# A ConvLSTM recurrence on one core: one sigmoid per half-step, and input products for row pairs

## The reference

```python
# layer 0: masked convolution, recurrence over the 16 image rows, skip
h = conv(x, w_i2s * mask)            # 1x3 kernel, 96 -> 192 channels, then a channel shuffle
for each image row:
    s = conv1d(_h, w_s2s) + h_row    # 1x3, 48 -> 192
    o, f, i, g = split(sigmoid(s), 4)
    c = f * c + i * g
    _h = o * tanh(c)
x = x + conv(out_h, w_skip * mask) + b_skip
# layer 1: tokens (16 x 256 x 96)
t = t + attention(layernorm(t))      # 6 heads of 16, causal, whole images of 256 tokens
t = t + moe(layernorm(t))            # 4 experts, hidden 384, gelu, the best 2 of 4
```

## Time and profile before

| | |
|---|---|
| median of three runs | 463.71 us |
| the profiled execution | 465.41 us, span 463.4 us |
| mean granted TensorE clock | 0.985 of full |
| PE busy | 436.8 us, 94% |
| PE weight loads | 347.5 us, 75% |
| DVE busy | 270.1 us, 58% |
| ACT busy | 263.8 us, 57% |
| POOL busy | 147.4 us, 32% |

### The profile page before, as it was taken

One profiled execution on the slowest core, in us unless ns is written; L12 is line 12 of the kernel. 1 busy time (PEld: TensorE's weight loads), 2 busy tenths in 40 slices (PEclk: granted clock), 3 DMA queues, 4 the chain that ended last, 5 costly groups with the idle time before them and its releaser, 6 DMA issues.

```text
span 463.4 us, 10793 instructions
## 1 busy us (share of the span) xinstructions
PE 436.8 (94%) x3186; PEld 347.5 (75%) x3186; DVE 270.1 (58%) x954; ACT 263.8 (57%) x740; POOL 147.4 (32%) x311
## 2 busy tenths in 40 slices
PE   6999998878799999999999999999999999999997
PEld 6999996445578777777786787678777876787776
DVE  3888888457417752774377348635852676166324
ACT  2544444246486648555855675576648664865370
POOL 5000000525503621553155315432542362245100
PEclk9999999969999999999999999999999999999899
DMA  8500000210021012101200210021002001200000
GB/s 211 124 0 0 0 0 1 64 39 18 25 47 35 0 40 52 31 0 46 54 20 0 52 50 17 0 59 43 17 7 75 20 0 34 54 16 1 18 2 18
DMA packets 14409, 14.95 MB, mean 32 GB/s; under 512 B 5426, under 2 KB 11316, under 8 KB 14388
## 3 DMA queue, kind: packets, MB, share of 16 engines
q1 hardware_dynamic: 13940, 14.15, 12.0%
q10 hardware_dynamic: 256, 0.39, 0.3%
q0 software_dynamic: 192, 0.15, 0.2%
HBM read 3.86 MB, written 1.57 MB: 12 GB/s over the span
## 4 chain that ended last, share of the span: by engine, by line
PE 75%; DVE 12%; ACT 6%; issue 4%; POOL 1%; DMA 1%; DVEq 1%; ACTq 1%; SPq 0%; POOLq 0%
PE F L1044 19%; PE T L1002 9%; PE A L1023 8%; PE F L1060 4%; PE F L1064 4%; PE S L986 4%; PE F L1061 3%; PE S L988 3%; PE F L1040 3%; PE S L991 2%; DVE c L647 2%; DVE ig L645 2%; ACT tc_sb L483 2%; DVE pt_sb L469 1%; PE M L965 1%
## 5 line engine op out<-in xcount | busy, mean ns | idle before, releaser
L420 POOL TENSOR_SCALAR p_sb<-p_sb,rden 128x128 f32<-128x128 f32 (+1 forms) x192 | 79.8, 430 | 130.8 <-DVE rden L728 128.6
L1044 PE MATMUL F<-w_sb,hid 128*128 128x96 f32 x768 | 102.3, 278 | 0.0
L1044 PEld LDWEIGHTS F<-w_sb,hid 128*128 128x128 f32 x768 | 94.7, 194 | 6.0 <-issue 6.0
L530 ACT ACTIVATE p_sb<-S,nmax 128x128 f32<-128x128 f32 (+1 forms) x192 | 78.9, 425 | 13.9 <-DVE nmax L722 13.8
L722 DVE TENSOR_REDUCE nmax<-S 128x2 f32<-128x512 f32 (+1 forms) x80 | 50.7, 633 | 48.7 <-PE S L991 48.4
L469 ACT COPY pt_sb<-T 128x512 f32<-128x512 f32 (+1 forms) x48 | 26.4, 550 | 68.5 <-PE T L1002 68.5
L576 ACT ACTIVATE hid<-F,b_sb 128x512 f32<-128x512 f32 x72 | 49.3, 686 | 8.1 <-PE F L1064 7.5
L1023 PE MATMUL A<-pt_sb,v_cur 128*32 128x128 f32 x576 | 44.2, 284 | 8.5 <-ACT pt_sb L469 4.5
L1002 PE MATMUL T<-id_sb,p_sb 128*128 128x128 f32 x288 | 49.4, 290 | 1.4 <-POOL p_sb L420 1.4
L1002 PEld LDWEIGHTS T<-id_sb,p_sb 128*128 128x128 f32 x288 | 30.9, 143 | 16.5 <-issue 13.9
L986 PE MATMUL S<-k_bd,q_st 96*128 96x384 f32 (+2 forms) x96 | 39.1, 414 | 3.2 <-DMA k_bd<-k_cur 2.5
(11 more groups left out here) (148 smaller groups left out, 794.3 us busy)
## 6 DMA issues: line engine op xcount, KB each, us to landing
k_bd<-k_cur SPq DMA_DIRECT2D x93, 32.0 KB, 2.0
q_st<-q_cur SPq DMA_DIRECT2D x28, 96.0 KB, 2.2
k_bd<-k_cur SPq DMA_DIRECT2D x93, 16.0 KB, 1.8
t_st<-t_cm SPq DMA_DIRECT2D x7, 192.0 KB, 2.4
out_y<-y_sb SPq DMA_DIRECT2D x7, 192.0 KB, 1.9
x_pad<-in_x SPq DMA_DIRECT2D x2, 612.0 KB, 8.7
w_sb<-in_w SPq DMA_DIRECT2D x1, 576.0 KB
hid<-in_w SPq DMA_DIRECT2D x1, 576.0 KB, 7.0
```

The source lines that it names most:

```text
L420: last = nc.gpsimd.tensor_scalar(p, p, rden[:, u % 3, i:i + 1], 1.0, ALU.mult, ALU.mult)
L530: last = nc.scalar.activation(p_sb[:, u % 3, i * nk:(i + 1) * nk], S[u % 2][:, i * nk:(i + 1) * nk], ACT.Exp, bias=nmax[:, u % 3, i:i + 1] ...
L1044: last = mm(dst[:, e * C:(e + 1) * C], hid[:, c, s * TT:(s + 1) * TT], w2_sb[:, c], start=False, stop=(c == NCH - 1), skip_group_check=True)
```

## The change

- The gate weights are rearranged while they are loaded, so that a PSUM bank holds g and i on partitions 0 to 47 (groups 0 and 1) and f and o on 64 to 111. This takes four DMAs for the input weights and four for the state weights, plus one for the skip weights; five of the nine are issued by ACT.
- ACT makes the gates of a half-step with one Sigmoid over 112 partitions and 256 columns, in place of two Tanh.
- DVE's part of a half-step is ig, fc, the cell and the two copies of h, all tensor_tensor without constants. fc, the cell and its tanh live on partitions 64 to 111.
- The skip is no longer DVE's: ACT copies it out of PSUM with the bias (`take_skip`), then POOL adds x to it (`add_input`).
- A bank now holds two rows of one half (`pair_bank`). The input's share is made for a pair of rows at once: for each of two gate groups and two taps three single-pass matmuls of 256 columns. For this x is split for each pair: ACT makes the high part (`high_inputs`), POOL the low part (`low_inputs`). The first pair is made in fp32 (`first_inputs`). The input weights are split once.

The diff, cut to its core:

```diff
+        def pair_bank(parity, hb):
+            return G[2 * parity + hb][0:GATE_M, :].rearrange("p (c r n) -> p c r n", c=2, r=2)
+        SWAPS = ((0, slice(FEAT, GATE_M), 0), (1, slice(0, 64), 1))
+        CROSS = ((0, slice(0, FEAT), 1, slice(64, GATE_M)), (1, slice(64, GATE_M), 0, slice(0, FEAT)))
 # sync
-            sp.dma_start(win_sb[:], w_input).then_inc(w_input_in, 16)
+            for blk, cols, blk_from in SWAPS:
+                sp.dma_start(win_sb[:, blk::2, cols], w_input[:, blk_from::2, cols]).then_inc(w_input_in, 16)
...
 # gpsimd
+            def low_inputs(p, parity):
+                pool.wait_ge(x_hi_done, p)
+                nc.gpsimd.tensor_tensor(x_lo[:, parity], pair_rows(p), as_f32(x_hi[:, parity]), ALU.subtract
+                                        ).then_inc(x_lo_done, 1)
+            low_inputs(1, 1)
...
+            def add_input(m, hb, row):
+                pool.wait_ge(skip_taken, m + 1)
+                dst = skip_out(row, hb)
+                nc.gpsimd.tensor_tensor(dst, dst, x_row(row)[:, hb * HALF:(hb + 1) * HALF, 1:], ALU.add
+                                        ).then_inc(t_half, 1)
+            def add_pair(p, parity, first=False, more=True):
+                if not first:
+                    for hb in range(2):
+                        add_input(4 * p - 2 + hb, hb, 2 * p - 1)
+                if more:
+                    low_inputs(p + 2, parity)
+                for hb in range(2):
+                    add_input(4 * p + hb, hb, 2 * p)
 # scalar
+            for blk, cols, blk_from, cols_from in CROSS:
+                act.dma_start(win_sb[:, blk::2, cols], w_input[:, blk_from::2, cols_from]).then_inc(w_input_in, 16)
...
-                nc.scalar.activation(t_fg[:, hb], v[64:64 + FEAT], ACT.Tanh, scale=0.5).then_inc(gates_tanh, 1)
-                nc.scalar.activation(t_ig[:, hb], v[0:FEAT], ACT.Tanh, scale=0.5).then_inc(gates_tanh, 1)
+                nc.scalar.activation(gate[:, hb], src, ACT.Sigmoid).then_inc(gates_done, 1)
...
+            def take_skip(m, hb, row):
+                act.wait_ge(skip_ready, m + 1)
+                nc.scalar.activation(skip_out(row, hb), K[hb][0:C, 0:HC].rearrange("p (b w) -> p b w", w=W), ACT.Identity,
+                                     bias=bsk_sb[:, 0:1]).then_inc(skip_taken, 1)
+            def pair(p, parity, first=False, more=True):
+                for r in range(2):
+                    for hb in range(2):
+                        m = 4 * p + 2 * r + hb
+                        cell_gates(m, hb, pair_bank(parity, hb)[:, :, r])
+                        if not (first and r == 0):
+                            take_skip(m - 2, hb, 2 * p + r - 1)
+                        if more and r == 0 and hb == 0:
+                            high_inputs(p + 2, parity)
+                        cell_out(m, hb)
...
+            act.wait_ge(x_in[2], 16)
+            pair(0, 0, first=True)
 # vector
+            def new_cell(m, hb):
+                dve.wait_ge(gates_done, m + 1)
+                V.tensor_tensor(ig[UP, hb], gate[LOW, hb, 0], gate[LOW, hb, 1], ALU.mult).then_inc(cell_dve, 1)
+                V.tensor_tensor(fc[UP, hb], gate[UP, hb, 0], cell[UP, hb], ALU.mult).then_inc(cell_dve, 1)
+                dve.wait_ge(cell_dve, 3 * m + 2)
+                V.tensor_tensor(cell[UP, hb], fc[UP, hb], ig[UP, hb], ALU.add).then_inc(cell_dve, 1)
...
+                V.tensor_tensor(h_pad[LOW, bs, 1:1 + W], o, t, ALU.mult).then_inc(h_ready, 1)
+                V.tensor_tensor(h_pad[UP, bs, 0:W], o, t, ALU.mult).then_inc(h_ready, 1)
 # tensor
+            def first_inputs(hb):
+                for c in range(2):
+                    for r in range(2):
+                        for tap in range(2):
+                            last = mm(pair_bank(0, hb)[:, c, r], wi_sb[:, tap, c], xr[:, r, bs, tap:tap + W], ...)
+                last.then_inc(gates_ready, 1)
+            def input_part(p, parity, hb, c, fresh=False):
+                if not fresh:
+                    pe.wait_ge(gates_done, 4 * p - 5 + hb)
+                if c == 0 and hb == 0:
+                    pe.wait_ge(x_lo_done, p)
+                for tap in range(2):
+                    for w, x_part in ((wi_hi, hi), (wi_lo, hi), (wi_hi, lo)):
+                        mm(pair_bank(parity, hb)[:, c].rearrange("p r n -> p (r n)"), w[:, tap, c],
+                           x_part[:, :, bs, tap:tap + W], ...)
...
+                        if not (first and r == 0):
+                            state_part(m, parity, hb, r)
+                            skip(m - 2, hb, fresh=first)
+                        if more:
+                            input_part(p + 1, 1 - parity, hb, r, fresh=first)
```

More of the change, by code:

```diff
@@ L42 @@
 STEPS = 2 * ROWS
+PAIRS = ROWS // 2
 E, HID = 4, 384
@@ L449, in body @@
                     x1_whole(n + 1)
+            def add_input(m, hb, row):
[3 more added lines that the diff above has]
+                                        ).then_inc(t_half, 1)
+            for i in range(4):
+                pool.wait_ge(x_in[i], 16)
+            def add_pair(p, parity, first=False, more=True):
[6 more added lines that the diff above has]
+                    add_input(4 * p + hb, hb, 2 * p)
+            add_pair(0, 0, first=True)
+            with pool.Fori(0, 2) as it:
+                add_pair(2 * it + 1, 1)
+                add_pair(2 * it + 2, 0)
+            add_pair(5, 1)
+            add_pair(6, 0, more=False)
+            add_pair(7, 1, more=False)
+            for hb in range(2):
+                add_input(STEPS - 2 + hb, hb, ROWS - 1)
             pool.wait_ge(w_in, 16 * N_WIN)
@@ new lines, in _ @@
+            act.wait_ge(w_dve, 1)
+            nc.scalar.copy(wi_hi[:], wi_sb[:]).then_inc(wi_hi_done, 1)
+            act.wait_ge(x_in[1], 16)
+            high_inputs(1, 1)
+            act.wait_ge(w_rec_in, 16 * N_WREC)
+            act.wait_ge(x_in[2], 16)
+            pair(0, 0, first=True)
+            act.wait_ge(x_in[3], 16)
+            with act.Fori(0, 2) as it:
+                pair(2 * it + 1, 1)
+                pair(2 * it + 2, 0)
+            pair(5, 1)
+            pair(6, 0, more=False)
@@ L495, in _ @@
+            pair(7, 1, more=False)
+            for hb in range(2):
+                take_skip(STEPS - 2 + hb, hb, ROWS - 1)
             act.wait_ge(w_in, 16 * N_WIN)
@@ L636, in split_expert_weights, with new_h @@
                 assert steps[0] == W_ALL
[L638 to L651, removed]
+            def new_cell(m, hb):
[4 more added lines that the diff above has]
+                V.tensor_tensor(cell[UP, hb], fc[UP, hb], ig[UP, hb], ALU.add).then_inc(cell_dve, 1)
+            def new_h(m, hb, first=False):
                 dve.wait_ge(cell_tanh, m + 1)
@@ L873, in split3 @@
                 return mm(dst, lo_l, hi_r, start=False, stop=stop, **kw)
-            def input_part(m, q, row, ready=False, fresh=False):
-                bs = slice(q % 2 * HALF, (q % 2 + 1) * HALF)
-                if not fresh:
-                    pe.wait_ge(gates_tanh, 2 * m - 6)
-                xr = x_row(row)
-                for c in range(2):
-                    for tap in range(2):
-                        last = mm(G[q][0:GATE_M, c * HC:(c + 1) * HC], wi_sb[:, tap, c], xr[:, bs, tap:tap + W],
-                                  start=(c == 0 and tap == 0), stop=ready, skip_group_check=True)
-                if ready:
-                    last.then_inc(gates_ready, 1)
```

150 lines of the change are left out of this document (75 added, 75 removed).

## The result

| | before | after |
|---|---|---|
| median | 463.88 us (4 runs, 463.58 to 466.24) | 471.55 us (4 runs, 471.01 to 471.74) |
| ratio, 95% interval | | 1.0162 [1.0134, 1.0191] |
| profiled execution | 465.41 us, span 463.4 | 471.51 us, span 469.6 |
| first token block's transposes | 80.06 us | 88.55 us |
| high part of the first expert input | 126.34 us | 134.02 us |

The kernel is 7.7 us slower, slower by more than 1%.

A forecast was written before the change was run, and what follows sets the result against it. The bound was the chain in which ACT and DVE hand one half-step to and fro, 2.23 us each. Without POOL's effect -5.4 us, with its 12.3 us +6.9, giving a median of 470.6 us; range 456 to 476.

The forecast's parts named there:

- case A: Recurrence: POOL's SBUF reads hold up DVE's two-input instructions; median 470.6 us, ends 465.2 to 477.0; chance 0.62.
- B: Recurrence: POOL's additions fall into DVE's gaps or DVE wins, so the effect is small; 458.3 us; chance 0.27.
- C: Recurrence: the low parts hold DVE up and the additions do not; 464.6 us; chance 0.09.
- The low part: POOL's low part of x, 6 times inside the recurrence: holds DVE up 1.05 us each, ends 0.9 and 1.36.
- DVE's chain without POOL: Recurrence: DVE's chain per half-step, 1.92 us plus 0.03 for the loop, is 1.95 against 2.23 before.
- ig to fc: DVE's chain: fc follows ig after 0.31 us as the partitions change; low end 0.20.
- POOL's term: Recurrence: 30 additions at 0.20 and 6 low parts at 1.05 cost 12.3 us, ends 6.9 and 18.7.
- PE: Recurrence: PE needs 1.82 us per half-step, 1.92 with restart, under DVE; split products of 256 columns 0.12 each.
- The start: Before the recurrence: first sigmoid waits for weights, products and x until 10.5 us (9 to 12.5); first ig at 10.9.
- The end: After the last h: product, ACT's copy and POOL's add take about 1.4 us against 1.34; nothing.
- D: Recurrence: sigmoid and tanh not in one table set, two reloads per half-step, 82 us, 546; chance 0.02.

The follow-up runs named there:

- run 2: The changed kernel with only the first low part made and used by all pairs; POOL's additions stay: 466.81 us, loop 66.32.
- run 3: The changed kernel without POOL's additions and low parts, so POOL does nothing in the recurrence: 460.83 us, loop 61.52.
- Run 5: The changed kernel with fc ahead of ig on DVE, nothing else: 467.66 us, loop 67.41.
- Run 7: The changed kernel with the pair's input products in fp32, no high and low parts of x or of the weights: 465.52 us, loop 66.62.
- run 6: The changed kernel with a one-element sigmoid as ACT's first instruction, ahead of the weights' cast: 471.34 us, loop 73.48.
- run 8: The changed kernel with the low part made by DVE in quarters between cell and h; POOL keeps the additions: 465.30 us, loop 65.16.
- run 10: The changed kernel with fp32 pair products, fc first, skip additions on DVE, no POOL work in the recurrence, no ACT skip copy: 457.65 us, loop 60.24.

## Why the prediction was right

The forecast was 470.6 us and case A, POOL's reads hold DVE up; measured were 471.55 and that case. Step by step:

- **Case A against B and C.** Shown. Taking away all that POOL reads gives 460.83; letting POOL only write, as long, gives 461.33. B, at 458.3, is 2.5 below where the kernel came out without the effect. C is refuted by run 2: against run 3 the additions alone cost 66.32 - 61.52 = 4.8 us, 0.16 each over 30 (forecast 0.20, ends 0.05 and 0.35).
- **The low part.** Forecast 1.05; in the changed kernel 1.03 by the sixth and seventh pair. Alone it costs (65.88 - 61.52) / 6 = 0.73, under my low end of 0.9. The two are not independent: 4.8 + 4.4 = 9.2, but together 72.74 - 61.52 = 11.2 (forecast 12.3). With the additions there, the low part falls on cell (1.32 us), where nothing covers it; without them on h (0.89 to 1.06), behind a tanh that covers some of it. 0.2 of the 11.2 is the half-step at the lower clock.
- **DVE's chain without POOL.** Forecast 1.95. The parts were right (ig to fc 0.32, cell to tanh 0.32), and the half-steps are 1.94 and 2.03; the loop costs 0.09 in every second half-step, 0.045 on the mean, where I had 0.03, and a half-step without it takes 1.94, where the parts made 1.92. 31 x 1.985 is 1.1 us more than forecast, POOL's term 1.1 less. The loop came out at 72.74 against 31 x 1.95 + 12.3 = 72.75, by two errors that cancel.
- **ig to fc.** The rule of the Trainium skill, "VectorE: DVE Perf Modes", section "Two Vector instructions with no wait between them", was weighed there. Run 5 is its test: an instruction whose inputs and output start in the same group of 32 partitions as the first input and the output before is not held. The copy of h to fc took 0.21, the copy of h to ig 0.32.
- **PE.** Forecast 1.82 to 1.92, under DVE: the products of 256 columns follow each other every 0.12 to 0.13 (51.96, 52.08, 52.21, 52.33), and the chain runs through DVE. Run 7 shows that the 0.16 won on PE had no taker.
- **The start, mis-sized.** The first ig came at 12.30, forecast 10.9. The wait for x ended where I put it, at 10.5. Its agreement is partly luck, as other runs have 9.98 to 11.34. The miss of 1.4 is a table load of 1.28 between that wait and the first sigmoid, for which the sum had no term. I counted one more load in all and put it at the end of the recurrence; that one came too (L635, at 101.63) and was hidden. The load for the cast at 4.08 made it three, but it is not what cost the 1.28: in run 7, without a cast, the one load still stands ahead of the first sigmoid, at 10.05. What takes it off the path is an earlier sigmoid, run 6. Run 6 shows that another wait stands close behind: of the 1.8 us by which the first ig came earlier, 1.08 were left at the transposes, and x had come 0.53 earlier in it.
- **The end.** Forecast nothing; from the end of h's last copy to the transposes +0.09. The last half-step, to the end of that copy, took 2.03, forecast 1.9: its cell was held up by an addition, and the sum had no term for that.
- **D** did not happen. The sigmoid and the tanh alternate 32 times and the trace has three loads to 120 us. That the Trainium skill, "ScalarE: Activation LUTs", section "Table sets: the hidden batching unit", lists tanh with the sigmoid agrees with it.

At the end of h's last copy the forecast was +6.9, measured 87.07 - 78.67 = +8.4: 1.4 from the start, 0.1 from the last half-step. That the median is off by only 1 us is in part luck: the shorter stretch at the lower clock behind it gave back 0.8 us, and nothing in the forecast or in the runs ties that to the change.

Where did the gain of the change go? Without what POOL reads the loop is 7.2 us shorter than before, and 4.8 of them are lost at the start (0.8 of it because x landed later in run 3 than in the changed kernel's execution); 2.5 are left at the transposes, about 3 in the median. POOL's reads cost 11.2 and turn that into the loss.

## What to carry to other kernels

An idle engine is not free room. Before work is moved to GpSimd, count the two-input VectorE instructions on the path that will run beside it: where they overlapped a GpSimd instruction that reads SBUF they ended some 0.15 us behind it, however short their own work. Here that cost 0.16 us for each short one (0.43 to 0.51 long, hit in nearly every half-step) and 1.03 for each long one (1.39). VectorE's own gap under a tanh took the same work, 0.30 to 0.35 us at a time, for nothing or next to nothing. And where the chain has one holder, a saving on another engine (here the split products on TensorE) buys nothing until the holder is moved.

## What the runs showed that I had not expected

- Two contended costs add to more than their sum (4.8 and 4.4 against 11.2), since the one moves the other to a worse place.
- A loop on VectorE can cost 0.09 us in the chain: tanh to h takes 0.43 instead of 0.34 at the first h of each turn (run 3 and the changed kernel). In run 8, whose turns hold two pairs, it stands at the first h of each pair in the loop, and in the three pairs written without a loop nowhere; so it comes with the loop's program, but what in it costs the time is not isolated. In run 10, where PE sets the pace, it does not show in the half-steps (1.96).
- A copy or cast as ScalarE's first instruction brought a table load of its own, 1.28 us, and the first sigmoid another. A single load is no help if it waits with the first sigmoid for the products (run 7, 10.05).
- The clock can drop in the recurrence too: 3.4 us at the lower level in the last pair of rows of one execution, and in none of the other profiled runs, with PE as little busy there. Why in that one stays open.
